# A two-layer correlation-and-convolution kernel: neighbours, turned rows and layer 1's weights placed anew, layer 0's maxima behind unit 0's affine, halves of units 1 to 4 on ScalarE

## The reference

```
norm = sqrt(sum(feature * feature, axis=1));  fn = feature / max(norm, 1e-12)
sims = [sum(fp[:, :, r:h + r, cc:w + cc] * fn, axis=1) for cc in range(5) for r in range(5)]
x = relu(einsum('bihw,oi->bohw', concat([feature, vol], 1), conv_w) + conv_b)
x = x + L0(gn(x));  x = x + L1(gn(x))
```

## Time and profile before

| | |
|---|---|
| median of 3 runs | 525.36 us (524.98 to 528.53) |
| the profiled execution | 528.95 us |
| its span, first to last instruction | 527.2 us |
| mean granted TensorE clock | 0.955 |
| TensorE busy | 446.3 us (85%) |
| VectorE busy | 373.2 us (71%) |
| ScalarE busy | 283.4 us (54%) |
| GpSimd busy | 124.8 us (24%) |

### The profile page before, as it was taken

One profiled execution on the slowest core, in us unless ns is written; L12 is line 12 of the kernel. 1 busy time (PEld: TensorE's weight loads), 2 busy tenths in 40 slices (PEclk: granted clock), 3 DMA queues, 4 the chain that ended last, 5 costly groups with the idle time before them and its releaser, 6 DMA issues.

```text
span 527.2 us, 13939 instructions
## 1 busy us (share of the span) xinstructions
PE 446.3 (85%) x5896; PEld 227.8 (43%) x5896; DVE 373.2 (71%) x869; ACT 283.4 (54%) x338; POOL 124.8 (24%) x179
## 2 busy tenths in 40 slices
PE   0457499278994998989898989898999989899996
PEld 0343245143542544545454545454545445444442
DVE  6789796686787668697868687877878796623322
ACT  1543255547355475856667575848475757523222
POOL 3534410131240311304031313131312203040400
PEclk9978789679896999999999999999999999999999
DMA  8271512522230245526657574132222315362432
GB/s 305 100 232 51 180 70 75 151 78 65 62 81 1 58 106 200 160 110 205 241 184 265 172 247 134 48 86 56 73 70 53 90 61 161 114 192 94 136 126 108
DMA packets 35013, 65.88 MB, mean 125 GB/s; under 512 B 12780, under 2 KB 22052, under 8 KB 34950
## 3 DMA queue, kind: packets, MB, share of 16 engines
q1 hardware_dynamic: 25158, 56.07, 32.2%
q0 software_dynamic: 9792, 8.92, 7.1%
HBM read 33.54 MB, written 28.87 MB: 118 GB/s over the span
## 4 chain that ended last, share of the span: by engine, by line
PE 40%; DVE 22%; ACT 18%; issue 7%; DMA 6%; SPq 3%; POOL 2%; DVEq 0%; ACTq 0%; POOLq 0%
PE conv_ps L579 27%; ACT v L681 8%; ACT operands L674 7%; PE gram_ps L504 4%; DVE operands L850 4%; DVE stats L803 3%; PE conv_ps L588 3%; DMA skew<-band_dram 3%; DVE nbr L899 2%; DVE xs L933 2%; ACT act_out L710 2%; PE gram_ps L517 2%; PE turn_ps L569 2%; SPq L362 2%; POOL v L444 1%
## 5 line engine op out<-in xcount | busy, mean ns | idle before, releaser
L579 PE MATMUL conv_ps<-operands,wh 128*128 128x512 f16 x1024 | 331.5, 386 | 0.3 <-DVE wl L921 0.3
L579 PE MATMUL conv_ps<-operands,wl 128*128 128x512 f16 x512 | 198.1, 387 | 0.0
L579 PEld LDWEIGHTS conv_ps<-operands,wh 128*128 128x128 f16 x1024 | 102.6, 100 | 122.4 <-issue 8.6
L710 ACT ACTIVATE act_out<-conv_ps,bias,wdown 128x512 f32<-128x512 f32 x128 | 97.0, 771 | 107.5 <-PE conv_ps L588 107.5
L933 DVE TENSOR_TENSOR xs<-xs,act_out 128x512 f32<-128x512 f32 x128 | 86.1, 686 | 49.2 <-ACT act_out L710 49.2
L850 DVE TENSOR_TENSOR operands<-v,operands 128x1024 f16<-128x1024 f32 x64 | 81.0, 1266 | 34.8 <-ACT v L681 28.3
L674 ACT ACTIVATE operands<-xs,affine 128x1024 f16<-128x1024 f32 x64 | 92.9, 1459 | 20.7 <-DVE affine L843 20.7
L803 DVE BATCH_NORM_STATS2 stats<-xs 128x6 f32<-128x512 f32 x128 | 79.9, 682 | 2.5 <-DMA xs<-in_x_dram 2.5
L579 PEld LDWEIGHTS conv_ps<-operands,wl 128*128 128x128 f16 x512 | 50.7, 99 | 57.0 <-issue 3.2
L681 ACT ACTIVATE v<-xs,affine 128x1024 f32<-128x1024 f32 x52 | 68.6, 1320 | 0.0
L296 POOL DMA_DIRECT2D mirror<-rows_dram x14 | 9.4, 675 | 233.6 <-DMA rows_dram<-rows 233.6
(11 more groups left out here) (70 smaller groups left out, 237.3 us busy)
## 6 DMA issues: line engine op xcount, KB each, us to landing
xs<-in_x_dram SPq DMA_DIRECT2D x32, 512.0 KB, 6.4
out_dram<-xs SPq DMA_DIRECT2D x32, 512.0 KB, 3.3
band_dram<-band SPq DMA_DIRECT2D x128, 60.0 KB, 1.9
skew<-band_dram SPq DMA_DIRECT2D x32, 222.5 KB, 3.1
vol<-corr_h POOLq DMA_DIRECT2D x48, 50.0 KB, 3.0
rows_dram<-rows SPq DMA_DIRECT2D x32, 65.8 KB
rows_dram<-rows SPq DMA_DIRECT2D x32, 63.3 KB
mirror<-rows_dram POOLq DMA_DIRECT2D x14, 110.9 KB, 2.5
```

What stands on the lines that cost most here:

```text
L579: pe.matmul(conv_ps[:, g % 4, :], w[:, l, t, m * P:(m + 1) * P], opnd[:, u % RING, part, t, n * HALF:(n + 1) * HALF], start=(t == 0 and w ...
L710: act.activation(in_rows(act_out[:, g % AOUT, :]), by_rows(conv_ps[:, g % 4, :]), ACT.Relu, bias=bias[:, l, m:m + 1], scale=wdown[:, l, m: ...
```

## The change

- **Neighbours.** For units 4 to 15 neighbours(k) and lengths(k) stand at j = 1 instead of 2 (norm_at): ahead of tile 2 of unit k + 1, not only of tile 3.
- **Turned rows.** rows_out_of_psum(k) stands at j = 4 on ScalarE, ahead of rectified(k - 1, 0); turn(k) stays at j = 5 on TensorE.
- **Band through DRAM.** The two banks go out together: four writes of 120 KB behind both banks, one semaphore, and both skews wait for all four.
- **Layer 0's weights.** The maxima come right behind unit_affine(0), ahead of unit 0's low tiles. ScalarE scales the weights, behind norm_tile(0, 3) and ahead of the bands. A sixth small instruction on VectorE puts the constant into wup.
- **Layer 1's weights.** The maxima come in slot 3 at j = 7 ahead of added(2, 3). ScalarE scales them in slot 4 ahead of deviations(5). The turns stand at j = 1, 2, 4, 5, 6; the fifth goes to turn_ps and waits for rows_out(4). High and low parts have places of their own. Unit 5 is now `ahead` as well: products(5, 0) at j = 7 of slot 4.
- **Halves.** For units 1 to 4 ScalarE makes the half, in norm_tile right behind the norm, once all products of the unit before are done and its own norm has finished; VectorE leaves it out. In units 3 and 4 that is ahead of exact_tile.

```diff
+        W1_MAX_SLOT, W1_SLOT, W1_MAX_AT = 3, 4, 7
+        W1_TURNED_AT = {1: 0, 2: 1, 4: 2, 5: 3, 6: 4}
+        W1_HIGH_AT = {0: 1, 3: 2, 4: 3, 6: 4}
+        W1_LOW_AT = {0: 0, 1: 1, 3: 2, 4: 3, 7: 4}
...
-            return valid(u) and u > STEADY and u != W1_SLOT + 1
+            return valid(u) and u > STEADY
+        def half_on_act(u):
+            return 0 < u <= STEADY + 1
+        def norm_at(k):
+            return 1 if ahead(k) else 2
...
+                sp.wait_ge(band_sb, BANKS * (k + 1))
+                for s in range(SPLIT):
+                    dst = bass.AP(band_dram, base + s * PART, [[PITCH, TILE], [BANK_GSZ, BANKS], [1, PITCH]])
+                    sp.dma_start(dst, band[s * TILE:(s + 1) * TILE, :, :]).then_inc(band_out, 16)
+                wait(sp, rn_step, RN_STEPS * k)
+                sp.wait_ge(band_out, 16 * SPLIT * (k + 1))
                 for n in range(BANKS):
-                    sp.wait_ge(band_sb, BANKS * k + n + 1)
-                    for s in range(SPLIT):
-                        dst = bass.AP(band_dram, base + n * BANK_GSZ + s * PART, [[PITCH, TILE], [1, PITCH]])
-                        sp.dma_start(dst, band[s * TILE:(s + 1) * TILE, n, :]).then_inc(band_out[n], 16)
-                wait(sp, rn_step, RN_STEPS * k)
-                for n in range(BANKS):
-                    sp.wait_ge(band_out[n], 16 * SPLIT * (k + 1))
                     src = bass.AP(band_dram, base + n * BANK_GSZ,
...
                 if l == 1:
                     pe.wait_ge(band_sb, BANKS * (W1_SLOT + 1))
-                    pe.wait_ge(w_low, W_LOWS + max(n - 1, 0))
+                    if n in (2, 3):
+                        pe.wait_ge(w_low, W_LOWS + n - 1)
+                    if n == KT:
+                        pe.wait_ge(rows_a, W1_SLOT + 1)
...
+            def scaled_weights(l):
+                act.wait_ge(w_step, W_STEPS * (l + 1))
+                for m in range(KT):
+                    act.activation(w_raw[l][:, m, :], w_raw[l][:, m, :], ACT.Copy, scale=wup[:, l, m:m + 1]
+                                   ).then_inc(w_scaled, 1)
...
+                if half_on_act(u):
+                    act.wait_ge(gram, BANKS * u)
+                    act.wait_ge(high, KT * u + t + 1)
+                    act.activation(half[:, t, :], opnd[:, u % RING, 0, t, :], ACT.Copy, scale=0.5
+                                   ).then_inc(halved, 1)
...
                 if valid(k + 1):
+                    if k == W1_SLOT:
+                        scaled_weights(1)
                     deviations(k + 1)
                     norm_tile(k + 1, 0)
                     exact_tile(k + 1, 0)
+                if k == W1_SLOT:
+                    high_weights(1, 0)
...
-                    if j == NORM_AT and valid(k):
+                    if valid(k) and j == norm_at(k):
                         lengths(k)
...
-                    if j == TURN_AT and valid(k):
+                    if j == TURN_AT - 1 and valid(k):
                         rows_out_of_psum(k)
...
+                dve.wait_ge(w_step, base + 4)
+                dve.tensor_scalar(wup[:, l, :], wup[:, l, :], W_SCALE, None, ALU.mult).then_inc(w_step, 1)
...
             unit_affine(0)
+            scale_weights(0)
             for t in range(KT):
                 low_tile(0, t)
                 half_tile(0, t)
-            scale_weights(0)
...
-                    if j == NORM_AT and valid(k):
+                    if valid(k) and j == norm_at(k):
                         neighbours(k)
+                    if k == W1_SLOT and j in W1_LOW_AT:
+                        low_weights(1, W1_LOW_AT[j])
...
+                    if k == W1_MAX_SLOT and j == W1_MAX_AT:
+                        scale_weights(1)
```

More of the change, by code:

```diff
@@ L200, in build @@
         band_sb = sem("band_sb")
-        band_out = [sem(f"band_out{n}") for n in range(BANKS)]
+        band_out = sem("band_out")
         skew_in = sem("skew_in")
@@ L222, in build @@
         VIEWS = 3 + QUARTERS
-        W_STEPS = 5
+        W_STEPS = 6
         W_HIGHS = KT + 2
@@ L263, in w_turned_at @@
                 return conv_ps[:, n, :]
+            if l == 1 and n == KT:
+                return turn_ps[:, 0, :]
             return gram_ps[:, n % 2, :]
@@ L269, in build @@
         TURN_AT = 5
-        NORM_AT = 2
-        W1_MAX_SLOT, W1_SLOT, W1_AT = 3, 4, 3
+        W1_MAX_SLOT, W1_SLOT, W1_MAX_AT = 3, 4, 7
+        W1_TURNED_AT = {1: 0, 2: 1, 4: 2, 5: 3, 6: 4}
+        W1_HIGH_AT = {0: 1, 3: 2, 4: 3, 6: 4}
+        W1_LOW_AT = {0: 0, 1: 1, 3: 2, 4: 3, 7: 4}
         HOLD = 1
         EARLY = 2
-        W_ON_POOL = (range(KT), range(KT))
         AHEAD_AT = 7
+        HALF_AT = GROUPS // 2
         def ahead(u):
-            return valid(u) and u > STEADY and u != W1_SLOT + 1
+            return valid(u) and u > STEADY
[3 more added lines that the diff above has]
+            return 1 if ahead(k) else 2
         def group_of(k, j):
-            u = k - 2 if j < 4 else k - 1
+            u = k - 2 if j < HALF_AT else k - 1
             return (u, (j + 4) % GROUPS) if valid(u) and u > 0 else None
@@ L631, in _ @@
                 for j in range(GROUPS):
-                    if k == W1_SLOT and j >= W1_AT:
-                        turn_weights(1, j - W1_AT)
+                    if k == W1_SLOT and j in W1_TURNED_AT:
+                        turn_weights(1, W1_TURNED_AT[j])
+                    if k == W1_SLOT + 1 and j == HALF_AT:
+                        pe.wait_ge(w_low, W_LOWS * LAYERS)
                     if j == TURN_AT and valid(k):
@@ L686, in band_out_of_psum @@
                 act.wait_ge(gram, BANKS * u + n + 1)
-                wait(act, band_out[n], 16 * SPLIT * u)
+                wait(act, band_out, 16 * SPLIT * u)
                 act.activation(band[:, n, :].rearrange("p (y e x) -> p y e x", e=TROWS, x=WCOLS),
@@ L715, in _ @@
                 norm_tile(0, t)
+            scaled_weights(0)
             for n in range(BANKS):
@@ L774, in _ @@
                 for j in range(GROUPS):
-                    if k == W1_SLOT and j >= W1_AT:
-                        high_weights(1, j - W1_AT)
-                    if j == NORM_AT and valid(k):
+                    if k == W1_SLOT and j in W1_HIGH_AT:
+                        high_weights(1, W1_HIGH_AT[j])
+                    if valid(k) and j == norm_at(k):
                         lengths(k)
@@ L853, in half_tile @@
             def half_tile(u, t):
+                if half_on_act(u):
+                    return
                 wait(dve, gram, BANKS * u)
@@ L1011, in _ @@
                 for j in range(GROUPS):
-                    if k == W1_SLOT and j >= W1_AT:
-                        low_weights(1, j - W1_AT)
-                    if j == NORM_AT and valid(k):
+                    if valid(k) and j == norm_at(k):
                         neighbours(k)
+                    if k == W1_SLOT and j in W1_LOW_AT:
+                        low_weights(1, W1_LOW_AT[j])
                     if j in (1, 2) and valid(k + 1):
```

14 lines of the change are left out of this document (3 added, 11 removed).

## The result

| | before | after |
|---|---|---|
| median | 526.37 us | 512.73 us (511.99 to 515.17) |
| ratio, with its 95% interval | | 0.9745 (0.9695 to 0.9796) |
| the profiled execution | 528.95 us | 511.99 us |
| its span | 527.2 us | 510.2 us |
| mean granted clock | 0.955 | 0.961 |

(The median of before is that of four runs here, one more than above.) The change saves 13.6 us by the medians and 17.0 by the two profiled executions. This is where the 17.0 lie, with the forecast's terms beside them. T(k) is the start of slot k.

A forecast was written before the change was run, and what follows sets the result against it. TensorE bounds the kernel, with a 1.6 us hole in each settled slot. Terms +4.5 - 9.7 - 13.5 - 0.7 + 1.0 give -18.4 us: 510.5 for the profiled execution, 507.0 as forecast from the median; range 502.5 to 513.5.

The forecast's parts named there:

- rival (a): VectorE and ScalarE in a ring become the bound; if merged writes save nothing, 0.8 us a slot lost: 513; chance 0.16.
- The hole: Settled slots: TensorE's 1.6 us wait for the neighbours goes when they move one step earlier, 1.5 us gained a slot.
- The correlation: Slots 7 to 10: it ends about when the second low tile wants to start, +0.25 us each, 1.0 in all.
- The skews: With merged band writes the second skew lands at slot start + 9.9, before the neighbours need it at about + 11.5.
- nsq idle for no DMA: Sign in a settled slot: VectorE's nsq, in the neighbours, waits for no transfer; wrong if it waits for skew in every slot.
- Slots 4 and 5: New placing of layer 1's weights: both slots together take 58.3 us instead of 68.0, -9.7.
- The halves: Halves on ScalarE at 1.15 us each: hidden in units 1 and 2, not in unit 3; +2.5 in slot 3.
- The start: Everything up to slot 4: slot 4 begins 4.5 us late.
- (b): Halves at 1.6 us each and turn 4 late by 2 more eat the start, +4: 511; chance 0.12.
- (c): Better than forecast: the halves hide and slot 4 begins on time, 4.5 us less: 502.5; chance 0.11.
- (d): Slower than before: skew lands at + 15.2, VectorE stands in the neighbours longer, +14 us: 539; chance 0.04.
- (e): The placing of layer 1's turns does nothing, turn 4 waits as turn 2 did: 513; chance 0.05.

The follow-up runs named there:

- short stores: The changed kernel with every store of the output cut to 64 of a tile's 1024 columns: 506.88 us, ratio 0.9595.
- Layer 0's pair: The changed kernel with layer 0's maxima behind the halves and GpSimd scaling, with one operation (519.44 us) and with two (515.22 us).

## Why the prediction was right or wrong

The forecast was 507.0 with a range of 502.5 to 513.5; 512.73 lies near its upper end, at rival (a)'s 513, and outside the 505 to 510 that had the chance 0.52. The kernel is faster by over 1%, as forecast with 0.93. The 5.7 us between forecast and median have three sources: the slots with stores lost 4.5 more than forecast, the start 2.9 less, and the step from the profiled execution to the median was off by 4.3 (slots 4 and 5 give 0.2). That the median is inside the range is in part luck: without the start's 2.9 it would be 515.6.

**The hole: right.** With the neighbours at step 2 again the hole of 1.6 us a slot is back; without, it is gone, with 0.3 to 0.8 of new waits at the averages (0.1 was taken). Slots 11 to 13 take 26.5 to 26.7.

**The correlation: right mechanism, mis-sized.** This is the step that failed, with the skews beside it. It was +0.25 in each of four slots; the five slots 6 to 10 took 137.9 - 5 x 26.6 = 4.9 us too much, and slot 14 another 0.3. Two of its numbers were off. Rows to correlation was read from slot 6 alone, 11.7 us, for all four slots. The trace of before had more in it; unit 7's rows, issued in slot 7, and its correlation in slot 8:

```profile
260.93 0.33 SPq L378 DMA_DIRECT2D rows_dram<-rows  x1
```

```profile
273.48 0.43 DVE L864 TENSOR_TENSOR mirror<-mirror,rn_own 100x256 f32<-100x256 f32 x1 [2.53 <-DMA rn_far<-rows_dram]
```

That is 12.55 us, and 12.56 for unit 8. After has 13.0 and 13.1 for these two. The other is the start of the rows: + 23.4 in slot 8 instead of + 21.3, because tile 3's store in front of them waits for an addition which the late correlation itself delays. The prediction costed one pass of that chain and not the ring. With short stores both shrink, and the excess falls from 4.9 to 0.9 us: shown to be the traffic. That the order alone does not cure it is shown too.

**The skews: 2.6 us too early.** The prediction added up 212.9 + 2.2 + 1.9 + 0.6 + 3.1 to + 9.9 and took them off the path. In slot 8 they landed at + 12.5. The writes start 1.0 later there than 212.9 had it, behind the stores of tiles 0 and 1; the last of the four is issued 2.9 us after the first (2.2 was taken) and lands 2.7 after its issue (1.9 was taken). So "nsq idle for no DMA" held in slots 7 to 13 but not in 6 and 14, nor in 15 (2.38 us; 4.60 before). The ring seems to start from the 0.72 us of slot 6; no run takes the skews' lateness away alone, so the 4.9 us are not divided between skews and rows.

**Slots 4 and 5: right to 0.2 us.** 58.1 against 58.3, with waits of 0.34 and 1.84 against 0.3 and 1.95, scaling in 2.6 of 2.7 us, and the clock at 1.00. Undoing the part gave back 9.1 to 9.5 of the 9.7 by the medians, 6.9 to 7.8 by the ratios.

**The halves: right place, too cheap.** One is 1.057 us against 1.15, but moving them back started slot 4 6.2 us earlier, where the prediction had 2.3 - 0.3 + 2.5 = 4.5 for them. Units 1 and 2 hide theirs, as said. The 2.5 for unit 4 was right, and so was the 2.3 for unit 3's tiles 2 and 3. What it left out are unit 3's tiles 0 and 1, whose halves stand ahead of the square root (1.2 at nsq), and the lower clock behind turn(3) (0.8).

**The start: 2.9 us better than forecast.** Put back as before one by one, the terms are +6.2 for the halves (4.5 forecast), +0.5 by slot 4's start or +1.2 by the turn's wait for the merged bands (+0.9 forecast), and -3.6 by slot 4's start or -2.3 by the volume of unit 0 for layer 0. That last one was undersized: -1.4 was taken, and only -0.85 of it carried as far as slot 3. By slot 4's start they add up to +3.1, and the trace has +1.6. The difference of 1.5 is no larger than the scatter of starts, and stays open.

**Profiled time against median.** The forecast for an execution like the profiled one was 510.5, and it measured 511.99: the misses of the start and of the slots nearly cancel. The remaining 4.3 us is the offset. Before's profiled execution was 3.6 above its then median, and I subtracted this as if it were the kernel's; after's lay 0.7 below its own. Both kernels scatter by 3 us from run to run (524.98 to 528.53; 511.99 to 515.17), so such an offset belongs to one execution, and a forecast on the median is not known better than that.

**The rivals.** (a), the ring, is what happened in slots 6 to 10, for 4 to 5 us where it was given 6. Its premise, skews at + 12.3, was met in the slots with stores (+ 12.5 to + 13.3), though the rows were later still in most of them; in slots 10 to 13 it was not. (b) was half right: the halves cost over what was summed, though not by taking 1.6 each, and slot 4's backlog did not come. (c) was near on the start (+1.6 against its 0), but not for its reason: the halves of units 3 and 4 did not hide, and layer 0's part gave more than was summed. (d) and (e) didn't occur.

## What to carry to other kernels

When a hole is closed, follow what leaves late round the whole ring, into the next repetition, and take the longest of the durations that the trace has for it in the slots with the same traffic, not the first one found. A small transfer on which a chain hangs is priced with the large ones beside it; putting it ahead of them moves the wait to the next small one in the queue. Work given to an engine that looks idle on the average is paid at the places where this engine stands on the chain: ScalarE's halves were free in two units and cost 6 us in two others. Count all instructions that are moved, also those ahead of the wait that is looked at.

## What the runs showed of the hardware

- **GpSimd's multiplication is slower with one operation than with two.** On 128x537 float32, a scale by a column took 1.654 us each, and 0.705 with a second multiplication by 1.0 in the same instruction. The two kernels differ in nothing else. Layer 0's pair shows the same, 6.46 us for four against 2.79.
- **The issue of a write lengthens with the traffic.** Four band writes took SyncE 2.01 us with short stores ahead of them and 3.35 with full ones (slot 8); in slot 12, where no stores leave, the four take 1.74. Eight of 60 KB took 5.89 in slot 6 before and four of 120 KB 3.14 after; in slot 8 it was 4.44 and 3.35.
- **The landing of a small transfer lengthens too:** the last views of slot 9 landed in 2.7 us with short stores and 4.1 with full ones. In slot 8 it was 3.1 and 4.2. The two kernels differ only in the bytes of the stores.
